# A post-norm decoder on one core: the expert rows are laid in PSUM ahead of the second layer, and two powers go ahead of two scatters

## The reference

```python
logits = x @ router_w
assignments = jnp.argmax(logits, axis=-1)
weights = probs at the assignment            # probs = softmax(logits)
hid = gelu(x @ w1[e] + b1[e])                # w1: 256 x 512
sel = hid @ w2[e] + b2[e]                    # w2: 512 x 256
x = _layernorm(x + sel * weights[:, None])   # (v - mean) / sqrt(var + 1e-5)
```

## Time and profile before

| what | value |
|---|---|
| median of 3 executions | 512.77 us (511.94 to 515.41) |
| the profiled execution: its time | 515.03 us |
| its span, from first to last instruction | 513.3 us |
| TensorE busy | 466.4 us, 91% of the span |
| VectorE busy | 345.9 us, 67% |
| ScalarE busy | 308.9 us, 60% |
| GpSimd busy | 217.1 us, 42% |
| mean granted TensorE clock | 0.966 of full speed |

### The profile page before, as it was taken

How to read it: one execution, slowest core, us unless ns; L and a number is a source line. 1 busy time by engine, 2 the same in 40 slices (tenths; PEclk the granted TensorE clock), 3 DMA queues, 4 the chain that set the end, 5 groups by cost and what they waited for, 6 DMA issues and landing times.

```text
span 513.3 us, 12715 instructions
## 1 busy us (share of the span) xinstructions
PE 466.4 (91%) x4461; PEld 400.7 (78%) x4461; DVE 345.9 (67%) x967; ACT 308.9 (60%) x1404; POOL 217.1 (42%) x299
## 2 busy tenths in 40 slices
PE   3687799998999999999999999989999998899991
PEld 2375587886877988878878978878889887899981
DVE  2779648856769767897578597685366636665653
ACT  2366647776768877877468585776475683333340
POOL 1365424462435544553236246543143432254443
PEclk9879789999999999999999999999999998999997
DMA  5762124435141323543151414060151393699900
GB/s 163 198 156 69 45 93 149 183 115 180 33 170 58 121 85 127 184 128 155 43 178 32 172 33 175 20 216 10 37 169 49 90 349 124 179 378 373 358 31 17
DMA packets 43804, 69.83 MB, mean 136 GB/s; under 512 B 12297, under 2 KB 33914, under 8 KB 43021
## 3 DMA queue, kind: packets, MB, share of 16 engines
q1 hardware_dynamic: 40344, 39.81, 24.8%
q10 hardware_dynamic: 926, 25.83, 13.5%
q0 software_dynamic: 2464, 3.31, 2.1%
HBM read 59.08 MB, written 29.77 MB: 173 GB/s over the span
## 4 chain that ended last, share of the span: by engine, by line
PE 71%; DVE 14%; DMA 6%; issue 3%; ACT 3%; POOL 2%; SPq 1%; DVEq 0%; POOLq 0%; ACTq 0%
PE bank L1418 26%; PE bank L1635 8%; PE bank L1492 7%; PE bank L1830 5%; PE bank L1819 5%; PE bank L1624 5%; PE bank L1664 4%; PE bank L1656 2%; PE bank L1601 2%; DMA vX<-v_tile 2%; DMA out_bias<-in_L_attn_out_b_dram 2%; ACT probs L1094 2%; DVE qk L1200 2%; PE bank L1451 2%; DVE rot L1198 2%
## 5 line engine op out<-in xcount | busy, mean ns | idle before, releaser
L1094 ACT ACTIVATE probs<-bank,neg_max 100x100 f32<-100x100 f32 x512 | 170.1, 369 | 35.6 <-DVE neg_max L1230 27.2
L996 POOL TENSOR_TENSOR probs<-probs,row_inv 100x400 f32<-100x400 f32 x128 | 112.7, 901 | 105.3 <-DVE row_inv L1235 105.1
L1094 ACT ACTIVATION_READ_ACCUMULATOR probs<-bank,neg_max 100x1 f32 x512 | 118.0, 230 | 0.0
L1230 DVE TENSOR_REDUCE neg_max<-bank 100x4 f32<-100x400 f32 x128 | 68.6, 564 | 10.8 <-PE bank L1624 5.4
L1635 PE MATMUL bank<-ident,probs 100*100 100x100 f32 x512 | 68.3, 256 | 6.3 <-POOL probs L996 4.6
L1635 PEld LDWEIGHTS bank<-ident,probs 100*100 100x100 f32 x512 | 51.0, 130 | 18.2 <-POOL probs L996 6.6
L1103 ACT COPY probsT<-bank 100x400 f32<-100x400 f32 x62 | 30.8, 496 | 42.5 <-PE bank L1635 36.5
L1242 DVE COPY probsT<-bank 100x400 f32<-100x400 f32 x66 | 37.6, 570 | 23.0 <-PE bank L1635 17.3
L1418 PE MATMUL bank<-cT_h,W_K 128*128 128x250 f32 (+1 forms) x224 | 46.6, 293 | 4.3 <-DVE kX L1157 1.7
L1492 PE MATMUL bank<-yT,W_Q 128*128 128x250 f32 (+1 forms) x224 | 50.1, 366 | 0.0
L1418 PE MATMUL bank<-W_O,oX_h 128*125 128x256 f32 (+1 forms) x224 | 43.8, 296 | 0.7 <-DVE oX_l L1252 0.7
(11 more groups left out here) (185 smaller groups left out, 964.9 us busy)
## 6 DMA issues: line engine op xcount, KB each, us to landing
expert_rows<-c_empty ACTq DMA_DIRECT2D x13, 1935.0 KB, 8.8
w<-in_L_ffn_w_dram SPq DMA_DIRECT2D x36, 512.0 KB, 7.3
vX<-v_tile SPq DMA_DIRECT2D x14, 200.0 KB
vX<-v_tile SPq DMA_DIRECT2D x12, 150.0 KB
xs<-in_x_dram SPq DMA_DIRECT2D x12, 125.0 KB
vX<-v_tile SPq DMA_DIRECT2D x12, 100.0 KB
kX<-in_L_xattn_WK_dram SPq DMA_DIRECT2D x2, 512.0 KB, 9.8
qX<-in_L_xattn_WV_dram SPq DMA_DIRECT2D x2, 512.0 KB, 6.4
```

Source lines behind the costliest of these rows:

```text
L996: probs_ready.mark(pool.tensor_tensor(v, v, r, ALU.mult), step)
L1094: i = act.activation(probs[:, k % SLOTS, w], sc_bank[p % 2 * 2 + u][0:T, w], ACT.Exp, bias=neg_max[:, k % SLOTS, h:h + 1], accum_out=row_s ...
L1230: max_ready.mark(dve.tensor_reduce(neg_max[:, k % SLOTS, :], src, AX_X, ALU.max, negate=True), step)
```

## The change

The norm of row + gate x (y + b2) equals the norm of row / gate + b2 + y, if eps is divided by the gate's square. The changed kernel computes the second form. The row carries 1 / gate in column D (the sum of the softmax, copied; 1.0 in an empty row). A new `lay_base(n)` on VectorE computes row x (1 / gate) + b2 and writes it into the PSUM bank of block n, and a second small operation computes eps / gate^2 (`eps_scaled`). The second layer's matmuls of blocks 2 and on then accumulate on top of what lies in the bank (no `start`), and the statistics and the result read the bank. For blocks 0 and 1, whose second layers are done in the first stage, the base goes to SBUF (`summed`) and the norm begins with an add of bank and base.

The base of blocks n and n+1 is laid at the head of a run of blocks; the base of block n+2 is laid after the norm of block n, for which `lay_base` waits on `res_ready`. TensorE's second layer waits on `base_ready` in place of `y_free`. On GpSimd the last two blocks of each run of blocks have both powers first and then both scatters.

```diff
+    empty_row[:, D] = 1.0
...
-                        dve.reciprocal(y2[w, slot:slot + k, D], gate_sum[w, two])
+                        dve.tensor_copy(y2[w, slot:slot + k, D], gate_sum[w, two])
...
             pe.wait_ge(gelu_ready, n + 1)
-            if n >= 2:
-                pe.wait_ge(y_free, n - 1)
+            pe.wait_ge(base_ready, n + 1)
             for f in range(FT):
-                i = pe.matmul(y_bank[n % 2][:, 0:D], hT[:, n % SLOTS_X, f, :], w[:, f, :], start=(f == 0), stop=(f == FT - 1))
+                i = pe.matmul(y_bank[n % 2][:, 0:D], hT[:, n % SLOTS_X, f, :], w[:, f, :], start=False, stop=(f == FT - 1), skip_group_check=True)
             i.then_inc(fc2_ready, 1)
...
+        def power(n):
+            pool.wait_ge(ve_ready, n + 1)
+            pool.tensor_tensor(rs[:, n % 2, :], ve[:, n % 2, :], half_power[:, :], ALU.pow).then_inc(rs_ready, 1)
+
+        def store(n):
+            x, s, count = x_of(n)
+            pool.wait_ge(s, count)
+            pool.wait_ge(res_ready, n + 1)
+            pool.indirect_dma_start(out=flat, out_offset=bass.IndirectOffsetOnAxis(ap=x[:, D + 1:ROW].bitcast(I32), axis=0),
+                                    in_=res[n % SLOTS_R][:, :], in_offset=None, bounds_check=B * T - 1, oob_is_err=False).then_inc(out_stored[n % SLOTS_R], 16)
+
         def run(blocks):
-            for n in blocks:
-                x, s, count = x_of(n)
-                pool.wait_ge(ve_ready, n + 1)
-                pool.tensor_tensor(rs[:, n % 2, :], ve[:, n % 2, :], half_power[:, :], ALU.pow).then_inc(rs_ready, 1)
-                pool.wait_ge(s, count)
-                pool.wait_ge(res_ready, n + 1)
-                pool.indirect_dma_start(out=flat, out_offset=bass.IndirectOffsetOnAxis(ap=x[:, D + 1:ROW].bitcast(I32), axis=0),
-                                        in_=res[n % SLOTS_R][:, :], in_offset=None, bounds_check=B * T - 1, oob_is_err=False).then_inc(out_stored[n % SLOTS_R], 16)
+            for n in blocks[:-2]:
+                power(n)
+                store(n)
+            for n in blocks[-2:]:
+                power(n)
+            for n in blocks[-2:]:
+                store(n)
...
-        def add_bias(n):
-            s = n % 2
+        def lay_base(n):
+
+            x, loaded, count = x_of(n)
             if n < NE:
                 b2 = b2r[:, n, :]
             else:
                 e = dve.value_load(expert_i[0:1, n - NE:n - NE + 1], min_val=0, max_val=NE - 1)
                 b2 = b2r[:, bass.ds(e, 1), :].rearrange("p o d -> p (o d)")
-            dve.wait_ge(fc2_ready, n + 1)
-            dve.tensor_tensor(biased[:, s, :], y_bank[s][:, 0:D], b2, ALU.add).then_inc(y_free, 1)
+            dve.wait_ge(loaded, count)
+            if n >= 2:
+                dve.wait_ge(res_ready, n - 1)
+            to = summed[:, n, :] if n < SEALED else y_bank[n % 2][:, 0:D]
+            dve.scalar_tensor_tensor(out=to, in0=x[:, 0:D], scalar=x[:, D:D + 1], in1=b2, op0=ALU.mult, op1=ALU.add).then_inc(base_ready, 1)
+            dve.scalar_tensor_tensor(out=eps_scaled[:, n % 2, :], in0=x[:, D:D + 1], scalar=EPS, in1=x[:, D:D + 1],
+                                     op0=ALU.mult, op1=ALU.mult).then_inc(eps_ready, 1)
 
         dve.wait_ge(b2_in, 32)
-        for n in range(SEALED):
-            add_bias(n)
...
+        def norm(n):
+            s = n % 2
+            y = y_bank[s][:, 0:D]
+            dve.wait_ge(fc2_ready, n + 1)
+            dve.wait_ge(base_ready, n + 1)
+            if n < SEALED:
+                dve.tensor_tensor(summed[:, s, :], y, summed[:, s, :], ALU.add).then_inc(y_summed, 1)
+                dve.wait_ge(y_summed, n + 1)
+                y = summed[:, s, :]
+            dve.bn_stats(st[:, s, :], y).then_inc(st_ready, 1)
+
+            dve.wait_ge(st_ready, n + 1)
+            dve.tensor_copy(waiter[0:1, 0:1], st[0:1, s, 0:1])
+            dve.bn_aggr(mv[:, s, :], st[:, s, :]).then_inc(mv_ready, 1)
+            dve.wait_ge(mv_ready, n + 1)
+            dve.wait_ge(eps_ready, n + 1)
+            dve.tensor_tensor(ve[:, s, :], mv[:, s, 1:2], eps_scaled[:, s, :], ALU.add).then_inc(ve_ready, 1)
+            dve.wait_ge(rs_ready, n + 1)
+            if n >= SLOTS_R:
+                dve.wait_ge(out_stored[n % SLOTS_R], 16 * (n // SLOTS_R))
+            dve.tensor_scalar(res[n % SLOTS_R][:, :], y, mv[:, s, 0:1], rs[:, s, :], ALU.subtract, ALU.mult).then_inc(res_ready, 1)
+
         def run(blocks):
+            for n in blocks[:2]:
+                lay_base(n)
             for n in blocks:
-                s = n % 2
-                x, loaded, count = x_of(n)
-                if n >= SEALED:
-                    add_bias(n)
-                dve.wait_ge(loaded, count)
-                dve.wait_ge(y_free, n + 1)
-                dve.scalar_tensor_tensor(out=summed[:, s, :], in0=biased[:, s, :], scalar=x[:, D:D + 1], in1=x[:, 0:D],
-                                         op0=ALU.mult, op1=ALU.add).then_inc(y_summed, 1)
-                dve.wait_ge(y_summed, n + 1)
-                dve.bn_stats(st[:, s, :], summed[:, s, :]).then_inc(st_ready, 1)
-
-                dve.wait_ge(st_ready, n + 1)
-                dve.tensor_copy(waiter[0:1, 0:1], st[0:1, s, 0:1])
-                dve.bn_aggr(mv[:, s, :], st[:, s, :]).then_inc(mv_ready, 1)
-                dve.wait_ge(mv_ready, n + 1)
-                dve.tensor_scalar(ve[:, s, :], mv[:, s, 1:2], EPS, None, ALU.add).then_inc(ve_ready, 1)
-                dve.wait_ge(rs_ready, n + 1)
-                if n >= SLOTS_R:
-                    dve.wait_ge(out_stored[n % SLOTS_R], 16 * (n // SLOTS_R))
-                dve.tensor_scalar(res[n % SLOTS_R][:, :], summed[:, s, :], mv[:, s, 0:1], rs[:, s, :], ALU.subtract, ALU.mult).then_inc(res_ready, 1)
+                norm(n)
+                if n + 2 in blocks:
+                    lay_base(n + 2)
```

More of the change, by code:

```diff
@@ L1713, in experts_block @@
     hT = sb("hT", [P, SLOTS_X, FT, P])
-    biased = sb("biased", [P, 2, D])
+    eps_scaled = sb("eps_scaled", [P, 2, 1])
     summed = sb("summed", [P, 2, D])
@@ L1732, in experts_block @@
     xT_taken = sem("xT_taken")
-    y_free = sem("y_free")
+    base_ready = sem("base_ready")
+    eps_ready = sem("eps_ready")
     y_summed = sem("y_summed")
```

## The result

Measured together with the kernel before, 16 runs each: 515.23 us median (513.30 to 518.11) against 512.53 (509.71 to 515.41). The ratio is 1.0064, with a 95% interval of 1.0044 to 1.0084, so the changed kernel is slower by 0.64% or 3.3 us (2.3 to 4.3); the two medians lie 2.7 us apart. The forecast was +3.0 us. The profiled execution has a span of 513.6 us and a time of 515.42.

The account below looks back on a forecast made before the run. TensorE was taken to bound the expert stage, VectorE and GpSimd the last 10 us. Pause +3.4, clock +1.7 and tail -2.1 made +3.0 us: 515.8 us against 512.77, with 8 in 10 between 513.2 and 518.3.

Parts of the forecast that it names:

- Which stage bounds: Expert stage: TensorE has no slack, so any delay before 494.70 arrives undiminished at the end.
- The pause, 3.4 us: Start of the expert stage: TensorE waits for block 2's base from 446.69 to 450.1, 3.4 us lost.
- the lower bound of 2.7 us: Smallest pause at the stage's start, if block 0's rows are there when VectorE has its tables.
- The clock, 1.7 us: After the pause: TensorE at half clock for 3.4 us, as after the pause near 127 us; 1.7 us lost.
- rival C: After the pause: clock low for 6.8 us, as at 62 us, all of it work; +4.7, 517.5 us; chance 0.16.
- The middle at nothing: Middle blocks: VectorE's 2.7 us and GpSimd's 3.0 per block stay below TensorE's 3.73, so no cost.
- The tail, 2.1 us: After block 16's second layer: last result 2.5 us earlier, 2.1 us gained, bounds 1.4 and 2.5.
- GpSimd's order: Tail: with both powers before both scatters, the last scatter starts at 506.0, 2.2 us ahead of 508.23.
- A: Stage's start: shorter pause of 2.7 us, clock held, 2.4 gained in the tail; +0.3, 513.1 us; chance 0.08.
- B: Stage's start: pause of 3.4 us as forecast, clock held; +1.3, 514.1 us; chance 0.16.
- D: Stage's start: block 2's base isn't late, only the tail's gain is left; -2.1, 510.7 us; chance 0.04.
- E: Norms shift against the weight transfers or the clock falls again; +6, 518.8 us; chance 0.06.

Follow-up runs that it names:

- e6: Kernel before plus one wait: block 2's second layer also waits for the result of block 1; nothing seeded. 1.0152 of the kernel before.
- e7: Kernel before plus one wait: block 2's second layer also waits for the result of block 0; nothing seeded. 1.0087 of the kernel before.
- e5: Changed kernel with 15 extra matmuls into an unused bank ahead of the wait for block 2's base. 1.0042 of the kernel before.
- e1: Changed kernel with GpSimd's old order, power and scatter of each block in turn to the end. 1.0097 of the kernel before.
- e4: Changed kernel with 28 extra matmuls into an unused bank ahead of the wait for block 2's base. 1.0069 of the kernel before.
- e3: Changed kernel with blocks 2 and 3 not seeded, four banks in turn, bases laid four blocks ahead. 0.9992 of the kernel before.
- e2: Kernel before with only GpSimd's new order, both powers and then both scatters. 1.0012 of the kernel before.
- e8: The same kernel as e3, measured again. 0.9972 of the kernel before.

## Why the prediction was right, step by step

- **Which stage bounds**: right. TensorE had no slack; what was lost at 446 arrived at the end, in the changed kernel as in e6 and e7.
- **The pause, 3.4 us**: right, 3.49 measured, and counted from the count matmul the second layer of block 2 starts 3.45 us later (9.03 against 5.58). The chain of VectorE took the steps given: 442.01 to 442.94 for the bases (1.0 forecast, 0.93 measured), 2.04 to the result (442.94 to 444.98), 0.52 to the base of block 2, 0.49 for it, 0.14 to TensorE. That the load of the rows, not the removed adds, sets its beginning was right in this execution. It is a near thing, as the lower bound of 2.7 us said: in e5 the rows were there in time.
- **The clock, 1.7 us**: the mechanism right, the size too small in the profiled execution: 2.66 (6.39 - 3.73). In e1, which has a pause of nearly the same length (3.38 us), the turn was 5.47 us, 1.74 more. The stretches of half a us tell the two apart. In e1 the clock fell only when TensorE was back at work, and was low for 3.4 us:

```profile
447.07 3.11 PE L1831 MATMUL bank<-w,hT 128*128 128x256 f32 x8 [3.38 <-DVE bank L1953]
```

```profile
447.50:448.00 0.50, 0.50 (x4) 0.73 1.08 358
...
451.00:451.50 0.50, 0.50 (x6) 0.85 1.12 356
```

  Read in this way, from the shares of the first and last stretch, the low clock of each kernel with a pause is:

| kernel | pause | low clock | of it with TensorE at work | half of that | turn longer by |
|---|---|---|---|---|---|
| changed | 3.49 | 6.8 | 5.3 | 2.65 | 2.66 |
| e1_old_pool_order | 3.38 | 3.4 | 3.4 | 1.71 | 1.74 |
| e6_only_wait_long | 4.89 | 6.8 | 3.3 | 1.64 | 1.69 |
| e7_only_wait_short | 1.89 | 3.4 | 3.4 | 1.70 | 1.73 |

  So what a pause costs on top of its length is half of the low time that TensorE works through, and both lengths that I had weighed, 3.4 us as at 127 and 6.8 us as at 62, come up. In the changed kernel the 6.8 us of rival C came, but the first 1.5 of them passed while TensorE stood anyway and cost nothing more. Why one execution has the short one and another the long one stays open. With e1's 1.74 the sum is 3.45 + 1.74 - 1.85 = 3.3 us, the timed difference; with 2.66 it is 4.3, near the 4.15 of the traces. The times would fit if most executions had the short one, but only the profiled executions show their clock. That the standing still brings the clock down is shown by e4 and e5, in which TensorE was kept busy and the clock stayed at 1.00.
- **The middle at nothing**: right, by e3, and in the changed kernel itself TensorE is busy for all of the 50.84 us from 446.13 to 496.97.
- **The tail, 2.1 us**: 1.85 measured. The last result ended 2.28 us earlier in relation to block 16's first norm operation (507.22 - 503.10 = 4.12 against 507.35 - 500.95 = 6.40), 2.5 forecast. The step that was mis-sized in this is the one on PSUM operands. I had taken an add as the measure for all of them. The statistics from the bank take 431 ns, no more than from SBUF, but the result does take more, by the view of the groups by form (from 446 us on):

```profile
L2001 DVE TENSOR_SCALAR res<-bank,mv,rs 128x256 f32<-128x256 f32 x16 | 8.7, 544 | 11.0 <-POOL rs L1905 11.0
L1957 DVE SCALAR_TENSOR_TENSOR bank<-xin,b2r 128x256 f32<-128x256 f32 x15 | 7.4, 493 | 3.0 <-DVE res L2001 1.6 <-issue 0.3
L1990 DVE BATCH_NORM_STATS2 st<-bank 128x6 f32<-128x256 f32 x16 | 6.9, 431 | 13.6 <-PE bank L1831 13.6
...
L2001 DVE TENSOR_SCALAR res<-summed,mv,rs 128x256 f32<-128x256 f32 x1 | 0.4, 413 | 0.7 <-POOL rs L1905 0.7
```

  544 ns from the bank, 413 from SBUF, in the same kernel: 0.13 each, 0.26 us for the two in the tail. The table of the Trainium skill ("VectorE: DVE Perf Modes", the section on the TRN2 errata) had given the prediction an estimate of the same 0.26 us by another split, 65 ns for each of four operations. This case's trace doesn't agree with the split: two of the four cost nothing (431 ns against 428 from SBUF in the kernel before) and two cost 131 ns. That the sums agree is luck. The right measure would have been an operation of the same kind with a PSUM source. The last scatter felt little of it, since it stands behind the scatter before it and not behind its own result.
- **GpSimd's order**: the last scatter 2.14 us earlier against 2.2 forecast, behind its neighbour by 1.34 us from start to start (1.32 forecast); e1 and e2 confirm the order's worth in the new kernel (0.95 us) and its lack of worth in the old. What the sum lacked is the landing, 2.72 us in place of 2.33. It isn't the same in all kernels with this tail: e3 and e8 have 2.70 and 2.72, e4 and e5 2.28 and 2.29, and the tails of e4 and e5 are 2.25 us shorter than before. Why it differs stays open.
- **Rivals**: A and B (clock held) didn't come, and e7 says that even a pause half as long brings the clock down here. D is what the traces of e3 and e8 show when the wait is really taken away. C is nearest to the profiled execution's +4.15. E didn't come: TensorE had no further wait in the middle and its clock did not fall again.

## What to carry to other kernels

Accumulating on a value laid into PSUM ahead of the matmuls moves work from behind the matmuls to a place ahead of them; that shortens the tail, but it turns "the bank has been read" into "the bank has been read, normed and written again", and the first turn of the pipeline pays for it (3.49 us of pause here, with two banks; none in e3 and e8, with four banks and two more blocks without a base in the bank). Give such a scheme its extra banks, or let the first blocks do without it.
A pause of the engine that bounds is dearer than its length: look at what the granted clock did after pauses of that size, and add it. And an order of two instructions in a queue has no worth of its own; it depends on how close together the work that feeds it comes.

## What was not expected of the hardware

A VectorE operation with two per-partition scalars (the result) takes 544 ns on 128x256 with its source in PSUM and 413 ns from SBUF, while statistics (431 against 428 ns) show no such difference. Writing a bank from VectorE costs 493 ns against 480 to 484 for the same form into SBUF. A pause of 1.89 us with TensorE at work around it cost 1.73 us more through the clock (e7), nearly as much again as the pause. The longer pause of e6, 4.89 us, cost no more through the clock (1.69 us), because half of its low stretch had passed before TensorE went back to work.
